# Spreading the rotation of queries and keys over the expert slots, and storing the keys once

## What is computed

```python
xn = layernorm(x)
out = x + attention(xn, W_q, W_k, W_v, W_o) + moe(xn, Wr, Wg, Wu, Wd)

# attention: 16 query heads of 16, 4 key/value heads, no mask
Qr, Kr = apply_rope(Q, positions), apply_rope(K_rep, positions)
#   pairs (x0, x1) -> (x0 cos - x1 sin, x0 sin + x1 cos)
weights = softmax(einsum('bhqd,bhkd->bhqk', Qr, Kr) / 4)
out = einsum('bhqk,bhkd->bhqd', weights, V_rep) @ W_o

# moe: 8 experts, top 2 of the router's logits, softmax over these two
h = einsum((clip(silu(x @ Wg[e]), -7, 7) * (x @ Wu[e])), Wd[e]);  out += h * w_e
```

## Time and profile before

| | |
|---|---|
| Median of 3 runs | 598.97 us (598.19 to 600.64) |
| The profiled execution | 597.43 us, span 595.7 us |
| TensorE, VectorE, ScalarE, GpSimd busy | 91%, 67%, 64%, 29% |
| Mean granted TensorE clock | 0.98 |
| SP's DMA queue | 40.26 MB, 22.8% of 16 engines |

### The profile page before, as it was taken

One profiled execution on the slowest core, in us unless ns is written; L12 is line 12 of the kernel. 1 busy time (PEld: TensorE's weight loads), 2 busy tenths in 40 slices (PEclk: granted clock), 3 DMA queues, 4 the chain that ended last, 5 costly groups with the idle time before them and its releaser, 6 DMA issues.

```text
span 595.7 us, 10552 instructions
## 1 busy us (share of the span) xinstructions
PE 539.9 (91%) x3288; PEld 265.4 (45%) x3288; DVE 401.5 (67%) x904; ACT 380.4 (64%) x548; POOL 173.1 (29%) x208
## 2 busy tenths in 40 slices
PE   1995756897999998999999999999999999999997
PEld 1832323454554554444444444444444444444433
DVE  4577756943666665787788787778877777874113
ACT  3421412332333335988988988898988988886562
POOL 3016744621222200031254232533164034400000
PEclk9997979998999999999999999999999999999999
DMA  9940244656632214015114104104115103000101
GB/s 293 376 152 9 89 148 156 188 178 187 169 107 67 62 42 105 25 34 125 31 44 125 35 19 124 53 19 125 36 36 124 36 19 89 19 3 20 45 27 54
DMA packets 38275, 53.54 MB, mean 90 GB/s; under 512 B 6145, under 2 KB 24449, under 8 KB 38241
## 3 DMA queue, kind: packets, MB, share of 16 engines
q1 hardware_dynamic: 31344, 40.26, 22.8%
q0 software_dynamic: 3408, 9.31, 5.7%
q10 hardware_dynamic: 3488, 3.55, 1.7%
HBM read 36.18 MB, written 16.65 MB: 89 GB/s over the span
## 4 chain that ended last, share of the span: by engine, by line
PE 71%; DVE 13%; DMA 5%; issue 4%; SPq 2%; POOL 1%; ACT 1%; DVEq 0%; ACTq 0%; POOLq 0%
PE bank L1248 17%; PE bank L1238 11%; PE bank L1240 10%; PE bank L1109 9%; PE bank L1173 7%; PE bank L1123 4%; DMA k_st<-rope_low 4%; PE bank L1190 3%; DVE xn_t L916 3%; PE bank L1272 3%; PE bank L1121 3%; SPq L382 1%; PE bank L1069 1%; DVE rope_a L849 1%; DVE xn L839 1%
## 5 line engine op out<-in xcount | busy, mean ns | idle before, releaser
L709 ACT ACTIVATE big<-bank 128x1024 f32<-128x1024 f32 x256 | 248.0, 1024 | 19.7 <-PE bank L1240 19.7
L1248 PE MATMUL bank<-big,v_st 128*32 128x512 f32 x1024 | 136.4, 605 | 0.0
L913 DVE TENSOR_REDUCE mx<-bank 128x1 f32<-128x512 f32 x128 | 88.3, 690 | 50.3 <-PE bank L1123 30.0
L664 ACT ACTIVATE xn_t<-bank 128x512 f32<-128x512 f32 x128 | 76.6, 599 | 45.3 <-PE bank L1111 41.5
L1238 PE MATMUL bank<-ms,ones_r 64*128 64x512 f32 x512 | 103.4, 400 | 0.4 <-ACT big L709 0.4
L1240 PE MATMUL bank<-qs,kb 64*128 64x512 f32 x512 | 101.1, 390 | 0.0
L908 DVE TENSOR_REDUCE mx<-bank 128x1 f32<-128x512 f32 x128 | 88.4, 691 | 17.1 <-PE bank L1111 14.5
L1173 PE MATMUL bank<-big,xn 128*128 x156 | 81.4, 647 | 17.5 <-ACT xn L678 16.9
L916 DVE CUSTOM_DVE_ANT_0 xn_t<-bank,xn_t 128x512 f32<-128x512 f32 x128 | 87.1, 681 | 0.0
L1109 PE MATMUL bank<-ka,qs 64*128 64x512 f32 x128 | 63.4, 495 | 10.3 <-DVE mx L916 7.9
L1109 PEld LDWEIGHTS bank<-ka,qs 64*128 64x128 f32 x128 | 23.4, 183 | 110.2 <-DVE mx L913 75.1
(11 more groups left out here) (141 smaller groups left out, 612.5 us busy)
## 6 DMA issues: line engine op xcount, KB each, us to landing
qs<-q_hl SPq DMA_DIRECT2D x64, 128.0 KB
rows_out<-xn SPq DMA_DIRECT2D x39, 128.0 KB, 2.7
ka<-k_st SPq DMA_DIRECT2D x16, 256.0 KB
kb<-k_st SPq DMA_DIRECT2D x16, 256.0 KB
xs<-in_L_attn_x SPq DMA_DIRECT2D x4, 512.0 KB, 6.6
big<-in_L_ffn_Wg SPq DMA_DIRECT2D x16, 128.0 KB, 6.4
big<-in_L_ffn_Wu SPq DMA_DIRECT2D x16, 128.0 KB, 6.6
big<-in_L_ffn_Wd SPq DMA_DIRECT2D x16, 128.0 KB, 6.5
```

The lines of the kernel that those rows point to most:

```text
L664: act.activation(gain[k % 2], mx_ps[i % 3], ACT.Relu).then_inc(gain_ready, 1)
L709: act.activation(probs[kt % 2][:, 2 * j:2 * j + 2, :].rearrange("p r q -> p (r q)"), st_ps[j][:, :], ACT.Exp, scale=1.0 / math.sqrt(HD)).t ...
L913: nc.vector.reduce_max(mx[h][:, STEPS + k, 1:2], mx_ps[i % 3], axis=X_AXIS).then_inc(mx_taken, 1)
L1248: last = mm(o_ps[32 * r:32 * (r + 1), :], v_st[p][:, kt, :], probs[kt % 2][:, r, :], start=(kt == 0), stop=(kt == KT - 1))
```

## The change

Parts are no longer in slots 0 to 11 but in slots 0, 2, 4, 6, 8, 10, 12, 16, 20, 24, 28 and 32. PARTS keeps its order, in which all parts of batch 0 lie among the first seven; the first load (step 15 of SP) waits for those only. ScalarE copies block 3's projections out of PSUM as well, ahead of slot 0, the keys to a new tile last_k. VectorE multiplies by cos for parts 3, 5, 7, 9 and 11. SHARED is 20. Keys are stored once as high and low (two DMAs in place of four), and ka and kb are put together by eight DMAs each, 64 KB a DMA, that read every row twice with a step of zero. Y stores are issued by SP in the step two behind their slot throughout.

```diff
-    k_st = nc.dram_tensor("k_st", [B, KV, STACK, 2, KCOLS], F32, kind="Internal").ap()
+    k_hl = nc.dram_tensor("k_hl", [B, KV, 2 * HD, 2, KCOLS], F32, kind="Internal").ap()
...
-        VECTOR_COS = (3, 5, 7)
+        VECTOR_COS = (3, 5, 7, 9, 11)
         AHEAD = 2
+        PART_SLOTS = (0, 2, 4, 6, 8, 10, 12, 16, 20, 24, 28, 32)
+        EARLY_PARTS = 7
+        FIRST_LOAD = 15
...
-        SHARED = 21
+        def part_at(t):
+            return PART_SLOTS.index(t) if t in PART_SLOTS else None
+        SHARED = 20
...
-                    for j, half in enumerate((rope_hi, rope_hi, rope_lo, rope_lo)):
-                        sp.dma_start(k_st[b, :, HD * j:HD * (j + 1), k % 2, :],
+                    for j, half in enumerate((rope_hi, rope_lo)):
+                        sp.dma_start(k_hl[b, :, HD * j:HD * (j + 1), k % 2, :],
                                      half[n][0:KV * HD, :].bitcast(F32)).then_inc(done, 16)
...
+            def twice(g, j, half, cols):
+                src = k_hl[g // KV, g % KV, HD * j:HD * (j + 1), half, cols]
+                return src.unsqueeze(0).to_broadcast([2, HD, cols.stop - cols.start])
             def load_ka(g, p):
-                src = k_st[g // KV, g % KV]
-                sp.dma_start(ka[p][0:STACK, :, :].bitcast(F32), src[:, :, QUART:KCOLS]).then_inc(ka_loaded[p], 16)
-                sp.dma_start(ka[p][STACK:P, :, :].bitcast(F32), src[:, :, 0:HALF]).then_inc(ka_loaded[p], 16)
+                for half in range(2):
+                    for j in range(2):
+                        low, high = 2 * HD * j, STACK + 2 * HD * j
+                        sp.dma_start(ka[p][low:low + 2 * HD, half, :].bitcast(F32),
+                                     twice(g, j, half, slice(QUART, KCOLS))).then_inc(ka_loaded[p], 16)
+                        sp.dma_start(ka[p][high:high + 2 * HD, half, :].bitcast(F32),
+                                     twice(g, j, half, slice(0, HALF))).then_inc(ka_loaded[p], 16)
             def load_kb(g, p):
-                for s in range(2):
-                    sp.dma_start(kb[p][STACK * s:STACK * (s + 1), :, :].bitcast(F32),
-                                 src[:, :, 0:HALF]).then_inc(kb_loaded[p], 16)
+                for half in range(2):
+                    for j in range(4):
+                        sp.dma_start(kb[p][2 * HD * j:2 * HD * (j + 1), half, :].bitcast(F32),
+                                     twice(g, j % 2, half, slice(0, HALF))).then_inc(kb_loaded[p], 16)
...
+            for t in range(SLOTS + 2):
+                q = part_at(t)
+                if q is not None:
+                    store_part(q)
+                n = t - FIRST_LOAD
+                if n == 0:
+                    for m in range(3):
+                        sp.wait_ge(qk_stored[m], sum(32 for o in range(m, EARLY_PARTS, 3)))
+                    load_ka(0, 0)
+                elif n == 1:
+                    load_q(0, 0, 0)
+                elif n in (2, 3):
+                    load_q(0, 1, 1, [n - 2])
+                elif n == 4:
+                    load_ka(1, 1)
+                elif n == 5:
+                    load_kb(0, 0)
+                elif n in (6, 7, 8, 9):
+                    load_q(1, (n - 6) // 2, 2 + (n - 6) // 2, [n % 2])
+                if t == SLOTS - 4:
+                    sp.wait_ge(mx_taken, taken(1, TURN))
+                    load_m(0)
+                if t >= 2:
+                    store_y(t - 2, (t - 2) % 4)
             for m in range(3):
                 sp.wait_ge(qk_stored[m], stored_before(NP + m))
...
             for q in range(AHEAD - 1):
                 high_part(q)
+            copy_projected(BLOCKS - 1)
+            for t in range(SLOTS):
+                expert(t, t % 2, first=t == 0, last=t == SLOTS - 1, beside=shared_with(t))
+                if part_at(t) is not None and part_at(t) + AHEAD - 1 < NP:
+                    high_part(part_at(t) + AHEAD - 1)
...
+            for t in range(SLOTS):
                 if t == SLOTS - SHARED:
-                    pe.wait_ge(ka_loaded[0], 32)
+                    pe.wait_ge(stacks_padded, 5)
+                    pe.wait_ge(pj_copied, 3 * BLOCKS)
+                    pe.wait_ge(ka_loaded[0], 128)
```

More of the change, by code:

```diff
@@ L101, in build @@
         rope_lo = [rope_low[:, m, :] for m in range(3)]
+        last_k = sb("last_k", [P, HALF])
         stats = [sb(f"stats{h}", [P, TB, 6]) for h in range(2)]
@@ L304, in vector_cos @@
         def vector_cos(q):
-            return PARTS[q][0] == BLOCKS - 1 or q in VECTOR_COS
+            return q in VECTOR_COS
         def projected(k, m):
-            if k == BLOCKS - 1:
-                return pj_ps[k][m]
-            return xn_t[k][:, m, :] if m < 2 else rope_hi[k][:, 0:HALF].bitcast(F32)
+            if m < 2:
+                return xn_t[k][:, m, :]
+            return last_k if k == BLOCKS - 1 else rope_hi[k][:, 0:HALF].bitcast(F32)
         def stored_before(q):
-            return sum(32 if PARTS[o][1] < 2 else 64 for o in range(q % 3, q, 3))
-        SHARED = 21
+            return sum(32 for o in range(q % 3, q, 3))
+        def part_at(t):
+            return PART_SLOTS.index(t) if t in PART_SLOTS else None
+        SHARED = 20
         def shared_with(t):
@@ L388, in store_y @@
                 sp.dma_start(rows_out[bass.ts(t, P), :], y_s[i]).then_inc(y_stored[i], 16)
[L390 to L395, removed]
             def load_q(g, h, i, heads=(0, 1)):
@@ L551, in _ @@
                 gather_rows(t)
-                q = t - 4 + AHEAD
-                if q < NP:
+                if part_at(t - 4) is not None and part_at(t - 4) + AHEAD < NP:
+                    q = part_at(t - 4) + AHEAD
                     if q >= 3:
@@ L642, in _, with copy_projected @@
             act.activation(gate_t[:, 1, :], gate_t[:, 0, :], ACT.Exp).then_inc(gate_exp, 1)
-            for k in range(BLOCKS - 1):
+            def copy_projected(k):
                 act.wait_ge(pj_ready, 3 * (k + 1))
@@ L647, in _ @@
                     act.activation(projected(k, m)[0:rows_m, :], pj_ps[k][m][0:rows_m, :], ACT.Copy).then_inc(pj_copied, 1)
+            for k in range(BLOCKS - 1):
+                copy_projected(k)
             act.wait_ge(hot_tile_ready, 1)
@@ L870, in rope_step @@
                     (k, m), n, rows_q = PARTS[q], q % 3, part_rows(q)
[L871 to L874, removed]
+                    dve.wait_ge(pj_copied, 3 * k + m + 1)
                     if q >= 3:
@@ L971, in _ @@
                     first_max(n)
-                take_y(t - 2, (t - 2) % 4, t % 2, 16 * ((t - 2) // 4))
+                if t >= 2:
+                    take_y(t - 2, (t - 2) % 4, t % 2, 16 * ((t - 2) // 4) if t >= 6 else None)
+                if part_at(t) is not None:
+                    rope_sum(part_at(t) + AHEAD)
+                    rope_step(part_at(t) + AHEAD)
             for t in range(SLOTS - 2, SLOTS):
@@ L1218, in _ @@
             to_columns(0, 0)
[L1219 to L1222, removed]
+            for t in range(SLOTS):
                 if t == SLOTS - SHARED:
-                    pe.wait_ge(ka_loaded[0], 32)
-                expert(t, t % 4, 16 * ((t + 1) // 4 + 1), last=t == SLOTS - 1, beside=shared_with(t))
+                    pe.wait_ge(stacks_padded, 5)
+                    pe.wait_ge(pj_copied, 3 * BLOCKS)
+                    pe.wait_ge(ka_loaded[0], 128)
+                expert(t, t % 4, 16 * ((t + 1) // 4 + 1), first=t == 0, last=t == SLOTS - 1, beside=shared_with(t))
             act_columns(SLOTS - 1, (SLOTS - 1) % 4)
@@ L1250, in values @@
                 last.then_inc(products_done, 1)
-            pe.wait_ge(kb_loaded[0], 32)
+            pe.wait_ge(kb_loaded[0], 128)
             pe.wait_ge(m_loaded[0], 64)
@@ L1292, in group @@
                                 if h == 0:
-                                    pe.wait_ge(ka_loaded[1 - p], 32 * ((g - p) // 2 + p) + 32)
+                                    pe.wait_ge(ka_loaded[1 - p], 128 * ((g - p) // 2 + p) + 128)
                             score_first(u + 2, ahead, 1 - p, kt, before_first(u + 2, kt))
@@ L1299, in group @@
                         if kt == KT - 1 and h == 1 and not last:
-                            pe.wait_ge(kb_loaded[1 - p], 32 * ((g - p) // 2 + p) + 32)
+                            pe.wait_ge(kb_loaded[1 - p], 128 * ((g - p) // 2 + p) + 128)
                             pe.wait_ge(m_loaded[0], 64 * (g + 2))
```

## The result

| | median | runs | against before |
|---|---|---|---|
| before | 599.34 us | 4 | |
| changed | 647.78 us | 4 (646.14 to 651.01) | 1.079, 95% interval 1.074 to 1.084 |

The profiled execution has a span of 646.4 us, 50.7 more than before. The forecast was 625 us, in 592 to 658. The way was right, and so was the place, but the terms for waiting, in attention and at slot 19, were too small.

A forecast was written before the change was run, and what follows sets the result against it. TensorE, busy 91% of a 595.7 us span, was taken as the bound. The expert stage gains 6 us and attention loses 32: span 622; adding 1.7 for the profiled execution and 1.5 for the median gives 625 us, range 592 to 658.

The forecast's parts named there:

- Engines per transfer: New ka and kb loads: outermost count 2 gives two DMA engines, at 24 GB/s each, 21.8 us for both.
- Rival one: ka and kb loads use all sixteen engines, so attention is unchanged and slot 19 isn't held: 579 us, chance 0.12.
- ms behind ka and kb: Attention: the maxima queue behind both loads, landing 24.7 us after kb's issue; TensorE stalls 3.9 us, six times, 23.4.
- 1.0 for the rest of q, gathers: Attention: 1.0 us within the 24.7 us from kb's issue until the maxima land, for remaining query loads and the mix's gathers.
- The clock: Attention: lowered TensorE clock behind each of six stalls adds 1.5 us, 9 us in all.
- SP's extra issues: Attention: sixteen issues for four, at 0.4 us, cost SP some 5 us more, hidden beneath the transfers.
- Slot 19: Expert stage, first shared slot: TensorE waits 7.3 us for the first ka and q, plus 1.6 for the clock.
- The y stores behind ka(1) and kb(0): Shared slots: y stores of slots 17 and 18 queue behind these loads, delaying VectorE: 3 us, plus 1.6 for the clock.
- The parts in shared slots: Four shared slots also hold a part, overrunning VectorE's free time: 4 x 1.5 = 6 us (0 to 10).
- The gain of the unshared slots: Slots 0 to 18: 57.4 us bare, plus 1.6 and 4, as ScalarE's 20 us of k-store waits go.
- the copies of block 3's projections: Ahead of slot 0 on ScalarE: three uncovered copies of 0.59 us add 1.6 us (0 to 2).
- The seven parts: Rotation in unshared slots 2 to 12 and 16: +0.6 us for each of seven, 4 us (0 to 12).

The follow-up runs named there:

- rows16: The changed kernel with each ka and kb load bringing 16 rows over both halves once, outermost count 16 in place of 2; 582.76 us, 0.972 of before.
- load14: rows16 with the first load of ka, and so q, one SP step earlier (14 in place of 15); 576.57 us, 0.965 of before.
- old_store16: The kernel before with the keys' memory layout turned round: stores have 64 rows outermost, loads read [4, 16, 2, 512]; 598.68 us, 0.997 of before.

## Why the prediction was right, and where its sizes were off

**Engines per transfer: right, to the number.** Two engines at 25 GB/s each; 24 had been taken. The profile of before was enough for it: one stretch of 2 us in which a store with four heads outermost moved at 25.3%. "DMA: Bandwidth & Descriptors" of the Trainium skill, section "Rules for kernel authors", names this very case, and here the trace agrees: 13.2% of 16 engines for the broadcast of two. Rival one, all sixteen engines, priced at 579, was not this kernel, but rows16 is that case: 582.8.

**ms behind ka and kb: right, mis-sized.** The sum had 24.7 us from kb's issue to ms landed. It was 26.3 in group 0 and 27.0 in the mean of the six groups, and the stalls were 5.95 us each and not 3.9. Two places show in group 0. The first is the start: the two engines are full only 2.5 us after kb's issue (DMA share 0.05 and 0.06 from 238.3 to 239.3 us, 0.13 from there), where 1.3 had been taken. The second is the term "1.0 for the rest of q, gathers": at 255.07 SP sends the next queries, and in the stretch behind that (columns as above)

```profile
256.50:258.00 1.50, 0.00 (x0) 0.00 (x0) 0.69 (x1) 0.59 (x1) 0.00 (x0) 1.00 0.75 210
```

210 GB/s at a share of 0.75 are 17.5 GB/s for each busy engine and not 25; the two loaded engines may share in that. An estimate from the bytes: some 0.26 MB were left for the two at 256 us and 0.18 MB were moved after 259, so they moved some 0.08 MB in these 3 us, where they move 0.15 undisturbed, a loss of 1.4 us. It takes for granted that the loads of queries are spread evenly over all sixteen. No run isolates either place.

The clock was put at 1.5 us a stall, 9 in all, and is 1.1 to 2.0, 9.3 in all: right. Stalls and clock are 45.0 together and not 32, attention as a whole 46.4: 14 of the 24 us by which the span (646.4) lies above the forecast's 622. SP's extra issues took 11 us and not 5 (kb and ka from 236.80 to 250.90, against 232.43 to 235.59 before); rows16 has the same issues and no wait for ms, so they do hide.

The other 10 us are in the expert stage, whose end came 4.3 us later than before and not 6 earlier.

**Slot 19: right place, half the size.** The wait was 13.5 us and not 7.3. ka's issue came at 116.4 and not 111: slot 0 began later, and SP first waits for the stores of part 6, sent in slot 12 (in rows16 the chain has 5.6 us for that, up to ka's issue at 114.0). The eight issues of 0.65 us, a y store and part 7 come before q on SP, and the sum took only the transfers' own time. Most of all, the last load of q(0) was issued at 126.95 and landed 12.8 us later: from 128 to 134 us all sixteen engines are full (share 1.04 to 1.07), with part 7's stores, the queries, y stores and gathers, where the sum had 5 us for q and part 7. What the order is worth shows in load14 against rows16. One step earlier brings ka forward by only 0.7 us, as both wait for part 6; but q now goes ahead of part 7's stores, its last load is issued 3.4 us earlier and lands after 3.0 us and not 5.6, and 5.9 us of waiting become 0.5.

**The y stores behind ka(1) and kb(0): right, small.** 5.6 us for 3. With it slot 25 is 8.5 us longer than its like (12.12 against 3.65), where 4.6 had been taken with the clock. Its clock is among that.

**The parts in shared slots: too dear.** 6 us had been set down for four slots. In rows16, where no y store waits, slot 25 takes 5.08 for 3.65, and the next, 28 to 30, sum to 12.9 for 12.2: some 2 us in all. The slots between are as short as without a part.

**The gain of the unshared slots: right.** 63.0 us had been worked out for nineteen; slots 0 to 17 took 60.4, and one more bare slot makes 63.4. Inside it the copies of block 3's projections cost 2.8 us and not 1.6: slot 0 takes 4.13 us for 2.99, and slot 1, at a granted clock of 0.63, 4.67 for 2.99. In load14 slot 1 takes 3.06, so the second loss doesn't always come. The seven parts are left with 3.2 of their 4 us.

**Not in the sum:** slot 0 begins 2.9 us later than before. In the other kernels it begins between 59.6 and 64.3, kernels with the same start included, so it is a difference between executions.

## What to carry to other kernels

Ask of each DMA what its outermost dimension counts on either side, and count dimensions whose steps fit together as one. A broadcast or a short list of heads put outermost takes engines away, and one 2 us stretch of the trace with its share shows it. Then ask not only who waits for the slow transfer but what is queued behind it: here loads that had twice the time they needed cost 45 us through 16 KB behind them. And stores, loads and the order of issue are one chain: each wait removed in the expert stage was given back at the next one until the first load was moved too.

## What the runs showed of the hardware that was not expected

Two saturated engines deliver 25 GB/s each, while sixteen together on the same 2 KB packets deliver 13.7 each; so by these rates kb and ka on two engines take 4.2 times what they took (21.0 us for 5.0), not 8. A burst on the others appears to slow these two as well; as said above, this is not shown. A stall of 5.4 to 6.7 us of TensorE cost 1.1 to 2.0 us more in the work behind it. And a 4 x 4 split of 16 evenly spaced rows doesn't limit a load to four engines, while the same count with a gap between the fours does (0.25 in old_store16).
